# A graph-network layer on one core: moving the on-chip tensors to other start addresses

## The chip, the cores and the metric

The kernel runs on one core of a Trainium2 chip. The metric is the device time of one execution, in microseconds (us). The engines are PE (TensorE; its weight loads are listed as PEld), DVE (VectorE), ACT (ScalarE), POOL (GpSimd) and SP (SyncE, which here only issues DMAs).

## The reference, cut to what matters

```python
h = jnp.maximum(_layernorm(x, axis=-1), 0.0)             # x: [128, 128, 128] f32
# one direction: h1 = h @ W.T ; g = h1 @ Wg.T
#   vals = (h1 + b) * sigmoid(g + bg);  sum over relations of (adj == rel) @ vals
out = fwd(adj, rels 2..40) + bwd(adj.T, rels 2..40) + loop(adj.T, rel 1)
x + relu(out)
```

The adjacency `adj` that is drawn holds only 0 and 1, so that only the loop direction with relation 1 contributes. The kernel computes that direction, sums up on the side how far `adj` is from 0 and 1, and has a general path behind a flag, which is not taken here.

## The kernel before

The 128 graphs (each 128 nodes by 128 features, float32) are worked in 32 groups of 4; two groups are one chunk of 512 KB of x and 512 KB of adj. All of x and all of adj stay on the chip (`x_all`, `adj_all`, 64 KB of each partition each).

The order is written out by hand, one queue for each engine, with semaphores:

- SP issues the loads in order: the first four graphs of x, the two weight matrices, the other four graphs of chunk 0, then x chunks 1 to 3 and adj chunk 0, then x and adj by turns; stores of finished chunks go in between from chunk 8 on. In HBM and in SBUF every run of a transfer is one row of a graph, 512 bytes.
- DVE computes the row statistics (L524), POOL the coefficients (L333, L336, and `rstd` with a power, L339) for batches of one, then two, then four groups. POOL and DVE share the normalisation to `xn` (L352, L541).
- PE transposes `xn` with `ident` (`turn_rows`, L751, 4 steps a group). ACT takes the relu to `hT_hi` (L414), DVE the remainder to `hT_lo` (L567).
- PE multiplies (`products`): for each graph `hT_hi` with `w_hi` (L764) and with `w_lo` (L765), then `hT_lo` with `w_hi` (L769), 12 steps a group, each 256 columns, onto a bias that ACT has put into PSUM (L421).
- ACT takes the sigmoid (L436), DVE multiplies to `vals` (L557), PE sums over the edges (`aggregate`, L786, mask by vals, which show as 8 steps a group), and DVE adds x (L582) in place.
- While it has nothing else to do at the start, PE multiplies `zeros` (`keep_busy`, L716, 256 columns of bf16).

In a PE step the first operand named (`hT`, `xn`, `mask`, `w_raw`) is loaded into the array, and the other (`w_hi`, `w_lo`, `ident`, `vals`, `w_gT`) streams through it. For `zeros` both come from the same tensor.

SBUF tensors are allocated one behind another in the order of the `sb(...)` calls. The program's first one, `x_all`, begins at byte 16,512 of each partition, 128 past a multiple of 4096. As `x_all`, `adj_all`, `xn`, `hT_hi`, `hT_lo`, `gate`, `vals` and `mask` are all multiples of 4096 bytes long, each of them begins 128 past a multiple of 4096. `stats` to `minus_half` take 1600 bytes together, so that `ident`, `ones`, `w_raw`, `w_gT`, `w_hi`, `w_lo`, `bias_all`, `zeros` and `bias_row` begin 192 past a multiple of 512. Every start is a multiple of 64.

Of the kernel before, what the change touches and what calls it, by code (L numbers as in the profile page):

```python
# [6 lines left out]
FP32, FP32R, BF16, INT32 = mybir.dt.float32, mybir.dt.float32r, mybir.dt.bfloat16, mybir.dt.int32  # L7
# [11 lines left out]
def build(nc, x, adj, W_fwd, W_bwd, W_loop, Wg_fwd, Wg_bwd, Wg_loop,  # L19
          b_fwd, b_bwd, b_loop, bg_fwd, bg_bwd, bg_loop, out):  # L20
    B, N, D = x.shape
# [6 lines left out]
    CC = CG * D  # L28
# [16 lines left out]
    with ctx:  # L45
        def sb(name, shape, dt=FP32):
            return ctx.enter_context(nc.sbuf_tensor(name, shape, dt))
# [3 lines left out]

        SIDE = max(B * D, 2 * NREL * D + 36 * D)
        x_all = sb("x_all", [128, SIDE])
        adj_all = sb("adj_all", [128, SIDE], INT32)
        xn = sb("xn", [128, XN, GC])
# [2 lines left out]
        gate = sb("gate", [128, 2, GC])  # L59
        vals = sb("vals", [128, 2, GC])  # L60
        mask = sb("mask", [128, MASKS, GROUP * N])
        stats = sb("stats", [128, BATCH_SLOTS, BATCH // 2, 6])
        var_eps = sb("var_eps", [128, BATCH_SLOTS, BATCH])
        rstd = sb("rstd", [128, BATCH_SLOTS, BATCH])
        mean_neg = sb("mean_neg", [128, BATCH_SLOTS, BATCH])
        minus_half = sb("minus_half", [128, BATCH])
        ident = sb("ident", [128, 128])
        ones = sb("ones", [128, 128])
        w_raw = sb("w_raw", [128, 2, 128])
        w_gT = sb("w_gT", [128, 128])  # L70
        w_hi = sb("w_hi", [128, 2 * D], FP32R)
        w_lo = sb("w_lo", [128, 2 * D], FP32R)
        bias_all = sb("bias_all", [128, 2, D])
        zeros = sb("zeros", [128, 4 * D], BF16)
        bias_row = sb("bias_row", [128, 2, D])
        junk = sb("junk", [128, 4, CC], BF16)
        dist = sb("dist", [128, CHUNKS])
        dist_sum = sb("dist_sum", [1, 1])
        flag = sb("flag", [1, 1], INT32)
# [61 lines left out]
        def view(side, cols):  # L141
            base = x_all[:, :] if side == "x" else adj_f32
            at = room[side]
            room[side] += cols
            assert room[side] <= SIDE
            return base[:, at:at + cols]
# [719 lines left out]
```

How the kernel before makes its waits and increments, by code:

```python
        @block.sync  # L241
# [21 lines left out]
            load_x(1)  # L263
            load_x(2)
            load_x(3)
            load_adj(0)
            for c in range(4, LOAD_AHEAD):
                load_x(c)
                load_adj(c - 3)
            for c in range(LOAD_AHEAD, CHUNKS):
                load_x(c)
                load_adj(c - 3)
                sp.wait_ge(out_ready, (c - LOAD_AHEAD + 1) * CHUNK)
                store_tile((c - LOAD_AHEAD) * CG, (c - LOAD_AHEAD) * CC, CG)
            load_adj(CHUNKS - 3)
            load_adj(CHUNKS - 2)
            load_adj(CHUNKS - 1)
            for c in range(CHUNKS - LOAD_AHEAD, CHUNKS - 2):
                sp.wait_ge(out_ready, (c + 1) * CHUNK)
                store_tile(c * CG, c * CC, CG)
            for g in range(GROUPS - 4, GROUPS - 1):
                sp.wait_ge(out_ready, g + 1)
                store_tile(g * GROUP, g * GC, GROUP)
            sp.wait_ge(out_ready, GROUPS)
            store_tile(B - GROUP // 2, (B - GROUP // 2) * D, GROUP // 2)
            sp.wait_ge(flag_ready, 1)
            with sp.If(sp.value_load(flag[0:1, 0:1], min_val=0, max_val=1) != 0):
                sp.wait_ge(stored, 16 * STORES)
                for d, (b_, bg_) in enumerate(((b_fwd, bg_fwd), (b_bwd, bg_bwd))):
# [10 lines left out]
                with sp.Fori(0, B) as b:  # L302
                    sp.wait_ge(g_stored, b * 16 + 16)
                    sp.dma_start(g_x, x[bass.ds(b, 1), :, :].rearrange("o n d -> n (o d)")
```

## Time and profile before

| | |
|---|---|
| median of 3 runs | 104.76 us (104.61 to 105.29) |
| profiled execution | 104.03 us |
| its span in the profile | 102.2 us, mean granted TensorE clock 0.992 |
| busy | PE 95.4, PEld 91.3, DVE 90.1, ACT 88.6, POOL 85.8 us |
| DMA | 25.45 MB, mean 249 GB/s |

The span goes from the first instruction to the last on the engines; 1.8 us of the execution lie outside it. Busy time is the time in which an engine had at least one instruction under way; steps of PE overlap, so that the distance between two starts is shorter than either step.

### The profile page before, as it was taken

What the parts mean: (1) busy time and instruction counts of PE and PEld (TensorE: products, weight loads), DVE (VectorE), ACT (ScalarE), POOL (GpSimd) and SP (SyncE); (2) the same over time, 40 slices, a digit from 0 to 9 for tenths busy, and PEclk for the clock granted to TensorE, in tenths of its full rate; (3) what the DMA queues carried; (4) which work ended last, traced back from release to release, by engine and by line L of the source; (5) the groups of instructions that cost most, each with busy time, mean ns of one, the idle gap of its engine ahead of it and who ended that gap; (6) DMA issues with size and microseconds to landing.
All of it is one profiled execution on the core that took longest, in us unless ns stands there. A gap on an engine that the chain in (4) does not pass through costs nothing.

```text
span 102.2 us, 2493 instructions
## 1 busy us (share of the span) xinstructions
PE 95.4 (93%) x802; PEld 91.3 (89%) x802; DVE 90.1 (88%) x196; ACT 88.6 (87%) x144; POOL 85.8 (84%) x162
## 2 busy tenths in 40 slices
PE   5986899998999999999999999999999999999960
PEld 2655789797999999999999999999999999999950
DVE  2289989999999999999999999999999788777761
ACT  5075498899799998999899989998999989898990
POOL 2188999999999999999999999999999999991000
PEclk9999999999999999999999999999999999999996
DMA  1899999999999999999999999999945150606345
GB/s 50 242 319 292 290 290 290 291 293 294 293 312 298 328 328 331 311 329 322 333 282 317 271 324 316 327 292 313 345 134 157 58 151 28 184 6 205 103 140 168
DMA packets 50288, 25.45 MB, mean 249 GB/s; under 512 B 866, under 2 KB 50276, under 8 KB 50276
## 3 DMA queue, kind: packets, MB, share of 16 engines
q1 hardware_dynamic: 50000, 25.17, 88.5%
q10 hardware_dynamic: 276, 0.13, 0.4%
q8 instruction: 6, 0.10, 0.4%
q14 instruction: 6, 0.05, 0.1%
HBM read 16.91 MB, written 8.39 MB: 247 GB/s over the span
## 4 chain that ended last, share of the span: by engine, by line
PE 71%; POOL 4%; ACT 3%; issue 1%; DVE 0%; POOLq 0%
PE psum L786 23%; PE psum L764 12%; PE psum L769 12%; PE psum L765 12%; PE psum L751 11%; POOL rstd L339 3%; ACT junk L442 2%; POOL xn L352 1%; ACT gate L436 0%; PE psum L811 0%; DVE dist_sum L628 0%; DVE flag L630 0%; POOLq L362 0%
## 5 line engine op out<-in xcount | busy, mean ns | idle before, releaser
L352 POOL TENSOR_SCALAR xn<-x_all,mean_neg,rstd 128x128 f32<-128x128 f32 x101 | 44.7, 454 | 0.7 <-POOL rstd L339 0.4
L764 PE MATMUL psum<-w_hi,hT_hi 128*128 128x256 f32 x128 | 33.8, 299 | 1.3 <-DVE w_lo L589 0.9
L786 PE MATMUL psum<-vals,mask 128*128 128x128 f32 x256 | 33.6, 275 | 0.1
L421 ACT ACTIVATE psum<-bias_all 128x1024 f32<-128x1024 f32 x32 | 33.1, 1035 | 0.3 <-DVE vals L557 0.3
L786 PEld LDWEIGHTS psum<-vals,mask 128*128 128x128 f32 x256 | 31.0, 191 | 0.2 <-issue 0.2
L765 PE MATMUL psum<-w_lo,hT_hi 128*128 128x256 f32 x128 | 31.0, 277 | 0.0
L524 DVE BATCH_NORM_STATS2 stats<-x_all 128x6 f32<-128x256 f32 x64 | 23.9, 418 | 3.2 <-DMA x_all<-in_x 3.0
L764 PEld LDWEIGHTS psum<-w_hi,hT_hi 128*128 128x128 f32 x128 | 24.1, 188 | 2.0 <-DVE w_lo L589 1.1
L557 DVE TENSOR_TENSOR vals<-psum,gate 128x512 f32<-128x512 f32 (+1 forms) x33 | 21.9, 663 | 3.9 <-ACT gate L436 3.3
L339 POOL TENSOR_TENSOR rstd<-var_eps,minus_half 128x16 f32<-128x16 f32 (+2 forms) x11 | 24.5, 2225 | 0.1
L765 PEld LDWEIGHTS psum<-w_lo,hT_hi 128*128 128x128 f32 x128 | 24.2, 189 | 0.0
L567 DVE SCALAR_TENSOR_TENSOR hT_lo<-psum,hT_hi 128x512 fp32r<-128x512 f32 x32 | 21.8, 682 | 1.2 <-ACT hT_hi L414 1.1
L414 ACT ACTIVATE hT_hi<-psum 128x512 fp32r<-128x512 f32 x32 | 19.2, 600 | 3.5 <-PE psum L751 3.5
L582 DVE SCALAR_TENSOR_TENSOR x_all<-psum,x_all 128x512 f32<-128x512 f32 (+1 forms) x33 | 21.7, 662 | 0.1
L436 ACT ACTIVATE gate<-psum 128x512 f32<-128x512 f32 (+1 forms) x33 | 19.4, 587 | 1.7 <-PE psum L769 1.7
L769 PE MATMUL psum<-w_hi,hT_lo 128*128 128x256 f32 x128 | 20.2, 278 | 0.0
L751 PE MATMUL psum<-ident,xn 128*128 128x128 f32 x128 | 19.5, 275 | 0.7 <-POOL xn L352 0.4
L442 ACT ACTIVATE junk<-adj_all,minus_half 128x1024 bf16<-128x1024 int32 x16 | 18.4, 1153 | 0.0
L769 PEld LDWEIGHTS psum<-w_hi,hT_lo 128*128 128x128 f32 x128 | 17.1, 188 | 0.1
L751 PEld LDWEIGHTS psum<-ident,xn 128*128 128x128 f32 x128 | 14.7, 142 | 1.5 <-POOL xn L352 0.8
L363 POOL CAST mask<-adj_all 128x512 f32<-128x512 int32 x22 | 13.3, 611 | 0.0
L541 DVE TENSOR_SCALAR xn<-x_all,stats,rstd 128x128 f32<-128x128 f32 x27 | 8.7, 340 | 0.0
(36 smaller groups left out, 31.3 us busy)
## 6 DMA issues: line engine op xcount, KB each, us to landing
adj_all<-in_adj SPq DMA_DIRECT2D x16, 512.0 KB, 6.8
x_all<-in_x SPq DMA_DIRECT2D x15, 512.0 KB, 6.8
out<-x_all SPq DMA_DIRECT2D x14, 512.0 KB, 6.2
out<-x_all SPq DMA_DIRECT2D x3, 256.0 KB, 2.3
x_all<-in_x SPq DMA_DIRECT2D x2, 256.0 KB, 3.0
out<-x_all ACTq DMA_DIRECT2D x1, 128.0 KB, 2.5
out<-x_all SPq DMA_DIRECT2D x1, 128.0 KB, 2.6
w_raw<-in_L_gnn_W_loop SPq DMA_DIRECT2D x1, 64.0 KB, 2.5
```

The lines of the kernel that those rows point to most:

```text
L339: pool.tensor_tensor(rstd[:, s, 0:n], var_eps[:, s, 0:n], minus_half[:, 0:n], ALU.pow).then_inc(rstd_ready, 1)
L352: last = pool.tensor_scalar(xn[:, g % XN, j * D:j * D + D], x_all[:, g * GC + j * D:g * GC + j * D + D], mean_neg[:, b % BATCH_SLOTS, k:k ...
L421: nc.scalar.activation(prod_ps[s].rearrange("p g a d -> p g (a d)"), bias_all[:, :, :].rearrange("p a d -> p (a d)").unsqueeze(1) .to_broa ...
L524: last = nc.vector.bn_stats(stats[:, b % BATCH_SLOTS, ((g - first) * GROUP + j) // 2, :], x_all[:, g * GC + j * D:g * GC + (j + 2) * D].re ...
L557: nc.vector.tensor_tensor(per_graph(vals[:, s, :])[:, some, :], prod_ps[s][:, some, 0, :], per_graph(gate[:, s, :])[:, some, :], ALU.mult) ...
L567: nc.vector.scalar_tensor_tensor(out=hT_lo[:, s, :], in0=hT_ps[s], scalar=0.0, in1=hT_hi[:, s, :].bitcast(FP32), op0=ALU.max, op1=ALU.subt ...
L582: nc.vector.scalar_tensor_tensor(out=cols, in0=sums_ps, scalar=0.0, in1=cols, op0=ALU.max, op1=ALU.add).then_inc(half_out if more else out ...
L751: last = nc.tensor.transpose(hT_ps[s][:, j * N:j * N + N], xn[:, g % XN, j * D:j * D + D], ident[:, :])
L764: nc.tensor.matmul(to, hi, w_hi[:, :], start=False, stop=False, skip_group_check=True)
L765: nc.tensor.matmul(to, hi, w_lo[:, :], start=False, stop=False, skip_group_check=True)
L769: last = nc.tensor.matmul(to, lo, w_hi[:, :], start=False, stop=True, skip_group_check=True)
L786: last = nc.tensor.matmul(to[:, j * D:j * D + D], mask[:, g % MASKS, j * N:j * N + N], vals[:, s, j * D:j * D + D], start=True, stop=True)
```

## The change

A tensor of 1920 bytes that nothing reads or writes is put in front, and nine small tensors are allocated right behind `mask` instead of behind the statistics, in another order. No instruction is added, removed or reordered.

```diff
         SIDE = max(B * D, 2 * NREL * D + 36 * D)
+
+        gap = sb("gap", [128, 480])
         x_all = sb("x_all", [128, SIDE])
         adj_all = sb("adj_all", [128, SIDE], INT32)
         xn = sb("xn", [128, XN, GC])
...
         mask = sb("mask", [128, MASKS, GROUP * N])
+        w_hi = sb("w_hi", [128, 2 * D], FP32R)
+        w_lo = sb("w_lo", [128, 2 * D], FP32R)
+        ident = sb("ident", [128, 128])
+        ones = sb("ones", [128, 128])
+        bias_all = sb("bias_all", [128, 2, D])
+        zeros = sb("zeros", [128, 4 * D], BF16)
+        w_raw = sb("w_raw", [128, 2, 128])
+        w_gT = sb("w_gT", [128, 128])
+        bias_row = sb("bias_row", [128, 2, D])
+        junk = sb("junk", [128, 4, CC], BF16)
         stats = sb("stats", [128, BATCH_SLOTS, BATCH // 2, 6])
         var_eps = sb("var_eps", [128, BATCH_SLOTS, BATCH])
         rstd = sb("rstd", [128, BATCH_SLOTS, BATCH])
         mean_neg = sb("mean_neg", [128, BATCH_SLOTS, BATCH])
         minus_half = sb("minus_half", [128, BATCH])
-        ident = sb("ident", [128, 128])
-        ones = sb("ones", [128, 128])
-        w_raw = sb("w_raw", [128, 2, 128])
-        w_gT = sb("w_gT", [128, 128])
-        w_hi = sb("w_hi", [128, 2 * D], FP32R)
-        w_lo = sb("w_lo", [128, 2 * D], FP32R)
-        bias_all = sb("bias_all", [128, 2, D])
-        zeros = sb("zeros", [128, 4 * D], BF16)
-        bias_row = sb("bias_row", [128, 2, D])
-        junk = sb("junk", [128, 4, CC], BF16)
         dist = sb("dist", [128, CHUNKS])
```

By these lengths `x_all` to `mask` and `w_hi` begin 2048 past a multiple of 4096 afterwards, `w_lo` and `w_raw` 3072 past, `ident` and `w_gT` on a multiple of 4096, and `ones`, `bias_all`, `zeros` and `bias_row` on multiples of 512. The statistics and `dist` stay on multiples of 64.

## Rows read from the trace of the kernel before

**Rows 1.** Busy time of each engine by stretch, granted clock, DMA share, GB/s.

```profile
0.00:2.50 2.50, 1.31 (x4) 0.49 (x5) 0.68 (x3) 1.28 (x1) 0.74 (x7) 1.00 0.14 44
2.50:3.70 1.20, 1.20 (x6) 0.71 (x5) 0.07 (x1) 0.00 (x0) 0.00 (x0) 1.00 0.84 244
3.70:5.40 1.70, 1.70 (x10) 1.35 (x8) 0.77 (x3) 0.07 (x1) 0.74 (x2) 1.00 0.87 255
5.40:12.90 7.50, 5.93 (x45) 4.70 (x44) 7.32 (x21) 4.41 (x10) 6.59 (x14) 1.00 1.18 300
12.90:24.60 11.70, 11.16 (x91) 10.32 (x89) 11.29 (x28) 10.98 (x18) 11.02 (x20) 1.00 1.20 292
24.60:45.00 20.40, 20.37 (x181) 20.37 (x182) 20.12 (x43) 19.43 (x33) 20.06 (x36) 1.00 1.12 314
45.00:67.00 22.00, 22.00 (x197) 21.95 (x196) 21.87 (x47) 21.36 (x35) 21.66 (x39) 1.00 1.06 313
67.00:95.00 28.00, 28.00 (x251) 27.99 (x250) 24.16 (x47) 26.84 (x43) 24.99 (x49) 1.00 0.57 165
```

**Rows 2.** Chain that ended last: shares of the span by line.

```profile
by line: PE psum L786 22.7%; PE psum L764 12.2%; PE psum L769 12.1%; PE psum L765 12.1%; PE psum L751 11.4%; POOL rstd L339 2.8%; ACT junk L442 2.1%; POOL xn L352 1.1%; issue 0.7%; ACT gate L436 0.4%; PE psum L811 0.2%; DVE dist_sum L628 0.
```

**Rows 3.** The same chain in time: start, us, what (products L764, L765 left out).

```profile
24.63 0.66 PE psum L751 x4
26.23 0.47 PE psum L769 x4
...
28.97 0.47 PE psum L769 x4
...
58.85 0.45 PE psum L769 x4
59.30 0.89 PE psum L786 x8
60.19 0.44 PE psum L751 x4
61.54 0.45 PE psum L769 x4
...
94.00 0.45 PE psum L769 x4
```

**Rows 4.** Timeline of PE: start, duration of the run of steps.

```profile
6.26 0.60 PE L716 MATMUL psum<-zeros 128*128 128x256 bf16 x4
...
51.90 0.60 PE L751 MATMUL psum<-ident,xn 128*128 128x128 f32 x4
```

**Rows 5.** Who waited for whom: total us, times, longest us.

```profile
POOL var_eps L333 <- DVE stats L524: 3.4, 2, 3.1
...
DVE stats L524 <- DMA x_all<-in_x: 3.0, 2, 2.1
```

**Rows 6.** Timeline of the start: POOL and DVE around the second load.

```profile
4.86 1.03 POOL L339 TENSOR_TENSOR rstd<-var_eps,minus_half 128x4 f32<-128x4 f32 x1
5.33 0.76 DVE L524 BATCH_NORM_STATS2 stats<-x_all 128x6 f32<-128x256 f32 x2 [0.94 <-DMA x_all<-in_x]
6.18 0.21 POOL L333 TENSOR_SCALAR var_eps<-stats 128x4 f32<-128x4 f32 x1 [0.29 <-DVE stats L524]
```

**Rows 7.** The page: GB/s in 40 equal slices, and the queue of all loads and stores (packets, MB, share of 16 DMA engines).

```profile
GB/s 50 242 319 292 290 290 290 291 293 294 293 312 298 328 328 331 311 329 322 333 282 317 271 324 316 327 292 313 345 134 157 58 151 28 184 6 205 103 140 168
...
q1 hardware_dynamic: 50000, 25.17, 88.5%
```

**Rows 8.** DMA issues: KB each, median us from issue to landing.

```profile
out<-x_all SPq DMA_DIRECT2D x1, 128.0 KB, 2.6
```

## Prediction

> **What bounds the kernel now.** I read the busy time by stretch first. In it PE is busy for 20.37 of 20.40 us, then 22.00 of 22.00, then 28.00 of 28.00: from 24.6 us to 95 us PE never runs dry [rows 1]. The chain of work that ended last says the same: 70.5% of the span lies on PE's five lines, 59.1% on those other than the transposes [rows 2]. The chain in time then gives the pitch, the distance from one PE step to the next. A whole group takes 61.54 - 58.85 = 2.69 us, of which 0.44 us are four transposes (0.110 each), 0.45 us the four products of L769 (0.113), 0.89 us the eight steps of L786 (0.111), and the 0.91 us that are left the eight products L764 and L765 (0.114) [rows 3]. There is a second pace: 28.97 - 26.23 = 2.74 us, with 0.47 us for L769, which is 0.1175 a step. Nineteen of the groups in the chain run at the shorter pace; the longer one rules up to 31 us and for two or three groups after a stall of PE. Neither pace follows the address: consecutive groups use the two halves of `hT`, 2048 bytes apart, and hold the same pace.
>
> Before 24.6 us the limit is another one. PE is busy 5.93 of 7.50 and 11.16 of 11.70 us, POOL 6.59 of 7.50 and 11.02 of 11.70 [rows 1]. Nothing but a load holds DVE in front (3.0 us, twice), and through it POOL, which waits 3.4 us for statistics and then has its own queue of powers and normalisations up to the start of the PE-bound stretch [rows 5]. So there are three stretches to price: the start, set by the first loads and then by POOL's queue; the middle, set by PE's pitch; and the end, set by the last store.
>
> **The change part by part.** The instructions, their order and their waits stay. What moves is the start address of every tensor. Each sort of access is one part.
>
> *PE reads.* Before, the streamed `w_hi` and `ident` begin 192 past a multiple of 512 and the loaded `hT`, `xn` and `mask` 128 past one; afterwards all begin on a multiple. If an off-multiple start cost time, steps that have one should be long. The transposes stream `ident` from 192 and load `xn` from 128, and have the shortest pitch of all float32 steps. Four of them take 0.60 us [rows 4]. Four steps that both load and stream `zeros`, from 192, take 0.60 us as well; they stream 256 columns of another type, half as many bytes. With 0.27 us for the last step both come to (0.60 - 0.27) / 3 = 0.11 us. The products are the only ones that stream 1024 bytes in a step, and no row has them at another alignment, so their 0.003 to 0.008 us above that pitch can't be cleared of the address altogether. Bounds: gain of all that lies above the transposes' pitch (rival A), loss of rival B. Between them I take zero, because the rows nearest to it, the transposes and `zeros`, show off-multiple starts at the shortest pitch.
>
> The Trainium skill (SBUF — State Buffer, terms and the note on cachelines) gives 16-byte lines and a penalty for each access that crosses into a new one; every start here is a multiple of 64 before and after. By it PE gains nothing; rival A would go against it. These rows can't separate lines of 16 bytes from longer ones.
>
> *DVE, ACT and POOL accesses.* The starts are multiples of 64 before and after, and in the middle all three are covered by PE. In the start POOL's queue is bare, some 18.4 us from 6.18 to 24.6: one part in a hundred on it would be 0.18 us. No row shows an address at work there; I take zero and keep 0.2 us each way for the range.
>
> *Loads.* `x_all` and `adj_all` move from 128 past a multiple of 256 onto one. In the middle no engine waits for a load, so what is gained there lies under PE. In the start it counts. The load of the other four graphs of chunk 0 ends DVE's wait at 5.33 us; DVE's statistics (0.76 us) end POOL's wait at 6.18 us [rows 6]. POOL had been free since 4.86 + 1.03 = 5.89 us, so 0.29 us can go at once, and more if the first load, which sets that 5.89, comes earlier too. Up to that load 640 KB come in (256, 64, 64, 256). At the 290 GB/s at which the queue runs from 10 to 24 us that is 2.26 us; at 345 GB/s, the best slice of the page, 1.90 us [rows 7]. So the bound of the gain is 0.36 us. The other bound is no gain, as nothing in the trace shows a run of 512 bytes on a multiple. A loss would need a row with loads that suffer from such a start, and there is none; I allow 0.1 us. The queue's average packet took 0.885 x 16 x 102.2 us / 50,000 = 28.9 ns for its 512 bytes. I take 0.25 us, nearer to the gain: in the first 5.4 us the rate is only 244 to 255 GB/s [rows 1], so part of this time is latency that stays. POOL's queue hands such a shift on in full, being filled without a pause up to 24.6 us, and PE hands it on from there.
>
> The rule behind that choice is in the Trainium skill (DMA: Bandwidth & Descriptors, how a descriptor splits into AXI transactions): transactions start on multiples of 256 bytes, and a start between them fetches bytes that go unused. Worked out from it, an estimate: 512 bytes from 128 past a multiple cost 20 beats, from a multiple 16. If the whole packet shrank so, those 2.26 us would become 1.81 us and the gain 0.45 us, before POOL's 0.29 us of slack cuts it. Whether that rule governs writes into SBUF no row shows.
>
> *Stores.* The last one is 128 KB and lands after 2.6 us [rows 8]. At 290 GB/s its bytes are 0.45 us, at 345 GB/s 0.38 us: up to 0.07 us. I take 0.05 us. The earlier stores have landed by then.
>
> *Sum.* On the profiled execution, 104.03 us: 0 - 0.25 - 0.05 gives 103.7 us. The median of the runs is 0.73 us above that execution, so on the median 104.76 - 0.3 = 104.4 us (rounded down).
>
> **The rivals.** *A, PE's pitch falls.* For it: PE is the bound, and the products, whose streamed operand is the longest in bytes, are the slowest steps. Lines L764, L765 and L769 hold 36.4% of the span in the chain, 37.2 us, in 27 groups of 12 = 324 steps, 0.115 us each. At the transposes' 0.110 us they would give back 1.6 us. L786, 22.7% or 23.2 us in 208 steps, 0.1115 each, gives 0.3 us more. With the start's 0.3 us that is 102.5 us; with half of it 103.4 us. Against it: off-multiple starts at the shortest pitch, as shown. From about 0.7 us of it the change is faster by over 1%.
>
> *B, slower: the two operands of a product collide.* Before, `hT` and `w_hi` begin at 128 and 192, so load and stream are 64 bytes apart in phase; afterwards both begin 2048 past a multiple of 4096. If the load and the stream of a step share something by address, steps lose time. The price is bounded by the two paces seen: if the nineteen groups at 2.69 us fall to 2.74 us, that is 0.95 us, and if all 324 products lengthen by the same 0.0045 us, 1.5 us. Less the start's gain it gives 105.4 to 105.9 us. It decides (over 1%) when a product's mean pitch passes 0.119 us. Against it: in L786 `mask` and `vals` already begin at the same phase, 128 past a multiple of 4096, at 0.111 us, and `zeros` loads and streams from one tensor at 0.11.
>
> *C, nothing happens at all:* the loads aren't sped up either, or what they gain is lost to another wait in the start (ACT's for adj, POOL's own queue). Then 104.8 us, give or take the pace of PE: which groups hold 2.74 us changes with each stall, a few groups either way, 0.2 us.
>
> **How the numbers follow.** A run of this kernel can tell about 1% from no change, 1.05 us: said once here. The forecast (start and end gain, PE as it is) has 0.45, C 0.33, A 0.14 (half of it or more 0.12), B 0.08 (past 1% 0.07). The 0.02 of A and the 0.01 of B that are left are within 1%, as are the forecast and C. So faster 0.12, same 0.81, slower 0.07. The likeliest value is 104.4 us. The forecast and C cover 104.4 - 0.45 (all of the load term and POOL's 0.2) to 104.8 + 0.5 (the spread of the runs of before). The range is carried a little into A and B at their half prices: 103.5 to 105.5 us.
>
> **What would show it.** The groups at 2.69 us in the chain of the changed kernel: unchanged against A and B. L769's four steps: 0.44 us would be A, 0.47 us everywhere B. The mean of a queue packet below 28.9 ns and a higher rate between 5 and 24 us confirm the load rule; DVE's wait for x below 3.0 us and the first PE-bound transposes before 24.63 us confirm that it counts. I would be wrong if the products' pitch hangs on where 1024-byte streams begin, or if POOL's queue in the start grows or shrinks with the addresses.

## The result, and the profile after

The changed kernel takes 105.89 us (median of 7 runs, 105.38 to 106.21) against 104.76 us (7 runs); the ratio is 1.0087, 95% interval 1.0064 to 1.011. It is slower by 0.9% (the two medians by themselves lie 1.1% apart), where 0.3% faster had been forecast, and the time lies above the range of 103.5 to 105.5 us. The profiled execution took 106.07 us with a span of 104.3 us, 2.1 us more than the span of before. (Lines of `kernel.py` that stand behind the new allocation are numbered two higher: L764 is L766, L769 is L771.)

Busy time by stretch, columns as in [rows 1]:

```profile
2.50:3.70 1.20, 1.20 (x6) 0.71 (x5) 0.19 (x1) 0.00 (x0) 0.00 (x0) 1.00 0.78 229
3.70:5.40 1.70, 1.70 (x8) 1.27 (x6) 0.57 (x2) 0.00 (x0) 0.86 (x2) 1.00 0.88 256
5.40:12.90 7.50, 6.06 (x45) 4.77 (x44) 7.12 (x21) 5.29 (x11) 6.03 (x13) 1.00 1.14 342
12.90:24.60 11.70, 10.78 (x92) 10.35 (x90) 10.65 (x26) 9.31 (x16) 11.02 (x19) 1.00 1.15 348
24.60:45.00 20.40, 19.84 (x173) 19.65 (x172) 19.94 (x43) 19.14 (x31) 20.06 (x37) 1.00 1.08 317
45.00:67.00 22.00, 22.00 (x194) 22.00 (x192) 21.77 (x47) 21.10 (x35) 21.66 (x40) 1.00 1.07 315
67.00:95.00 28.00, 28.00 (x246) 28.00 (x245) 24.15 (x48) 26.60 (x43) 25.75 (x50) 1.00 0.39 117
```

PE is as full as before from 45 to 95 us, at the same granted clock, and yet gets through fewer steps: 246 instead of 251 from 67 to 95 us. The loads run at 342 and 348 GB/s where they ran at 300 and 292, but not in the first 5.4 us.

The chain that ended last, shares and then pieces in time, to set against [rows 2, 3]:

```profile
by line: PE psum L788 22.3%; PE psum L766 12.5%; PE psum L771 12.4%; PE psum L767 12.3%; PE psum L753 11.1%; POOL rstd L341 2.7%; ACT junk L444 2.1%; POOL xn L354 1.1%; issue 0.7%; ACT gate L438 0.4%; PE psum L813 0.2%; DVE dist_sum L630 0.
...
25.55 0.65 PE psum L753 x4
27.15 0.48 PE psum L771 x4
27.63 0.89 PE psum L788 x8
28.52 0.44 PE psum L753 x4
29.92 0.48 PE psum L771 x4
...
96.32 0.48 PE psum L771 x4
```

Here the 2.1 us can be read off. The first and the last piece with four products of `hT_lo` are 25 groups apart in both kernels: 96.32 - 27.15 = 69.17 us against 94.00 - 26.23 = 67.77 us, **1.40 us** more. That is 2.767 us a group in place of 2.711 on average. There is no short pace any more: four products take 0.48 us in all 26 pieces, while transposes (0.44) and edge sums (0.89) take what they took. The first such piece comes **0.92 us** later, and from the last one to the end it is 104.3 - 96.32 = 7.98 us against 102.2 - 94.00 = 8.2 us, **0.2 us** less. (The 1.40 us are net: the kernel before has 0.12 us of waits at two transposes in this stretch, the changed one none.)

The start, in the timeline (start us, duration us; the last bracket is idle time and what ended it), to set against [rows 6]:

```profile
5.78 0.76 DVE L526 BATCH_NORM_STATS2 stats<-x_all 128x6 f32<-128x256 f32 x2 [1.51 <-DMA x_all<-in_x]
6.63 0.21 POOL L335 TENSOR_SCALAR var_eps<-stats 128x4 f32<-128x4 f32 x1 [0.86 <-DVE stats L526]
12.45 2.06 POOL L354 TENSOR_SCALAR xn<-x_all,mean_neg,rstd 128x128 f32<-128x128 f32 x4 [0.18 <-POOL rstd L341]
13.67 1.16 DVE L543 TENSOR_SCALAR xn<-x_all,stats,rstd 128x128 f32<-128x128 f32 x4
14.60 0.30 POOL L335 TENSOR_SCALAR var_eps<-stats 128x8 f32<-128x8 f32 x1
```

The second load of x ended DVE's wait at 5.78 us, 0.45 us later than before, and POOL's queue (its second run of `var_eps`) began 0.45 us later with it. The other 0.47 us arise inside POOL's queue, mostly between 12.45 and 14.98 us: four pieces of a normalisation take 2.06 us where the kernel before has this:

```profile
11.98 1.74 POOL L352 TENSOR_SCALAR xn<-x_all,mean_neg,rstd 128x128 f32<-128x128 f32 x4 [0.18 <-POOL rstd L339]
13.59 1.10 DVE L541 TENSOR_SCALAR xn<-x_all,stats,rstd 128x128 f32<-128x128 f32 x4
13.80 0.20 POOL L333 TENSOR_SCALAR var_eps<-stats 128x8 f32<-128x8 f32 x1
```

There POOL is done at 13.72 us, 0.13 us after DVE has begun; after the change DVE begins 0.84 us before POOL is done. The queue's share of the page and the time to landing of the last store, to set against [rows 7, 8]:

```profile
q1 hardware_dynamic: 50000, 25.17, 81.1%
...
out<-x_all SPq DMA_DIRECT2D x1, 128.0 KB, 2.3
```

A packet took 0.811 x 16 x 104.3 us / 50,000 = 27.1 ns instead of 28.9.

### The profile page after: what moved, and what is told of

The parts are those of the page before. It is cut to its first block, busy times and chain, and to the rows that moved or that the text cites. A ratio compares the mean times of both kernels' runs of the same rounds, so it can differ in the third digit from the quotient of the medians.

```text
span 104.3 us, 2493 instructions
## 1 busy us (share of the span) xinstructions
PE 97.0 (93%) x802; PEld 93.0 (89%) x802; DVE 90.7 (87%) x196; ACT 88.8 (85%) x144; POOL 86.1 (83%) x162
## 4 chain that ended last, share of the span: by engine, by line
PE 71%; POOL 4%; ACT 2%; issue 1%; DVE 0%; POOLq 0%
PE psum L788 22%; PE psum L766 12%; PE psum L771 12%; PE psum L767 12%; PE psum L753 11%; POOL rstd L341 3%; ACT junk L444 2%; POOL xn L354 1%; ACT gate L438 0%; PE psum L813 0%; DVE dist_sum L630 0%; DVE flag L632 0%; POOLq L364 0%
## 5 line engine op out<-in xcount | busy, mean ns | idle before, releaser
L766 PE MATMUL psum<-w_hi,hT_hi 128*128 128x256 f32 x128 | 34.6, 304 | 0.9 <-DVE w_lo L591 0.6
L788 PE MATMUL psum<-vals,mask 128*128 128x128 f32 x256 | 33.7, 275 | 0.2 <-issue 0.2
L767 PE MATMUL psum<-w_lo,hT_hi 128*128 128x256 f32 x128 | 32.0, 282 | 0.0
L766 PEld LDWEIGHTS psum<-w_hi,hT_hi 128*128 128x128 f32 x128 | 24.2, 189 | 1.5 <-DVE w_lo L591 0.9
L771 PE MATMUL psum<-w_hi,hT_lo 128*128 128x256 f32 x128 | 20.7, 283 | 0.0
L771 PEld LDWEIGHTS psum<-w_hi,hT_lo 128*128 128x128 f32 x128 | 17.7, 192 | 0.0
L543 DVE TENSOR_SCALAR xn<-x_all,stats,rstd 128x128 f32<-128x128 f32 x27 | 9.2, 361 | 0.0
```

The lines of the kernel that those rows point to most:

```text
L766: nc.tensor.matmul(to, hi, w_hi[:, :], start=False, stop=False, skip_group_check=True)
L767: nc.tensor.matmul(to, hi, w_lo[:, :], start=False, stop=False, skip_group_check=True)
L771: last = nc.tensor.matmul(to, lo, w_hi[:, :], start=False, stop=True, skip_group_check=True)
L788: last = nc.tensor.matmul(to[:, j * D:j * D + D], mask[:, g % MASKS, j * N:j * N + N], vals[:, s, j * D:j * D + D], start=True, stop=True)
```

## The experiments

The pace of a group is worked out for each as above, from the first and the last piece of four products in the chain, divided by 25, so that it has in it what PE waits in between; ratios are against runs of the kernel before on the same chip at that time, whose median was 104.31 to 104.76 us.

### Which half of the change, and by what

`again` is the changed kernel once more.

> The changed kernel once more. Known so far: a group of PE steps takes 2.77 us (before: 2.69 or 2.74), four products of hT_lo take 0.48 us (before 0.45 or 0.47), and the stretch that PE bounds begins at 25.5 us (before 24.6). If the pitch belongs to the addresses, the pitch is 0.48 us again in every group. Whether the later start belongs to them too: if it does it begins near 25.5 us again, if it is chance it can be anywhere from 24.5 us on. Time 105.4 to 106.2 us.

Measured: 105.68 us, ratio 1.0131 (1.0083 to 1.0179). The pace is 2.767 us again and 0.48 us in every piece: it belongs to the addresses. POOL's queue began at 6.16 us this time, as before the change, so the 0.45 us of the late load are chance; from there to the first piece of four products (26.59 us) it was 20.43 us, after the change 27.15 - 6.63 = 20.52 us, before 26.23 - 6.18 = 20.05 us. So 0.4 us of the late start are in both traces of this kernel; they come back below, under the start.

That the late load is scatter shows in all the traces: POOL's queue began between 6.16 and 6.75 us in the sixteen with `x_all` moved by the 1920 bytes, and at 6.18 and 6.79 us in the two without.

`gap_only` is the first half of the change alone, `order_only` the second.

```diff
# gap_only, against the kernel before
+        gap = sb("gap", [128, 480])
         x_all = sb("x_all", [128, SIDE])
# order_only, against the changed kernel
-        gap = sb("gap", [128, 480])
         x_all = sb("x_all", [128, SIDE])
```

> Only the 1920 bytes in front, the small tensors in the old order: x_all to mask begin on multiples of 2048, w_hi, w_lo and ident 64 past a multiple of 512. Theory P (the loaded and the streamed operand of a product collide when they begin at the same phase): they are 64 apart, so the short pitch, 0.45 us for four products, about 1.5 us less than the changed kernel, 104.3 us. Theory S (a stream of 1024 bytes that begins on a multiple of 512 is slower by itself): short pitch too, 104.3 us. Theory D (the faster loads, whose targets are now on multiples of 256, disturb PE's reads): the long pitch, 0.48 us, and 105.9 us. All: loads at 340 GB/s or more from 6 to 20 us.

> Only the new order, without the 1920 bytes: everything from x_all to bias_row begins 128 past a multiple of 512, so loaded and streamed operand of a product have the same phase, but none is on a multiple. Theory P: long pitch, 0.48 us for four products, 105.9 us or above. Theory S: short pitch, 0.45 us. Theory D: short pitch, since the loads are as before, near 290 GB/s from 6 to 20 us; for S and D 104.8 us.

`skew64` puts 64 unused bytes ahead of `w_hi` (16 elements; the others called skew likewise).

```diff
+        skew = sb("skew", [128, 16])
         w_hi = sb("w_hi", [128, 2 * D], FP32R)
```

> The changed kernel with 64 more unused bytes ahead of w_hi, so that w_hi to bias_row begin 64 past a multiple of 512 and x_all to mask stay. Theory P and theory S: short pitch, 0.45 us for four products, about 104.3 us. Theory D: long pitch, 0.48 us, 105.9 us.

Measured: `gap_only` 104.35 us (ratio 0.9983, 0.9955 to 1.0011), `skew64` 104.36 us (0.9983, 0.9958 to 1.0008), `order_only` 106.19 us (1.0188, 1.0112 to 1.0264). The chain of `gap_only`:

```profile
90.82 0.44 PE psum L752 x4
92.17 0.45 PE psum L770 x4
...
94.86 0.45 PE psum L770 x4
```

and of `order_only`, with its busy time from 12.9 to 24.6 us:

```profile
92.08 0.44 PE psum L752 x4
93.47 0.48 PE psum L770 x4
...
96.24 0.48 PE psum L770 x4
```

```profile
12.90:24.60 11.70, 11.02 (x93) 10.57 (x92) 10.90 (x26) 10.31 (x17) 11.02 (x20) 1.00 1.20 291
```

94.86 - 92.17 is 2.69 us, 96.24 - 93.47 is 2.77 us. `order_only` has nothing on a multiple of 512 and the old rate of loads, and has the long pace in every group; so neither theory S nor theory D holds. What it shares with the changed kernel is the distance, 0. The whole loss of pace comes from the reordering, none from the 1920 bytes.

### Which tensor

`w64_only` moves `w_hi` and `w_lo` by 64 bytes and puts 448 more behind `w_lo`, so that all that follows moves by 512 and keeps its phase. `rest64` leaves the two where they are and puts the 64 bytes behind them.

```diff
# w64_only, against the changed kernel
+        skew = sb("skew", [128, 16])
         w_hi = sb("w_hi", [128, 2 * D], FP32R)
         w_lo = sb("w_lo", [128, 2 * D], FP32R)
+        back = sb("back", [128, 112])
         ident = sb("ident", [128, 128])
# rest64
         w_lo = sb("w_lo", [128, 2 * D], FP32R)
+        skew = sb("skew", [128, 16])
         ident = sb("ident", [128, 128])
```

> The changed kernel with only w_hi and w_lo moved 64 bytes on; ident, ones, bias_all, zeros and the rest stay on multiples of 512. Theory P (the loaded and the streamed operand of a product collide when they begin at the same phase): short pitch, 0.45 us for four products in most groups, about 104.3 us. Theory R (it is another of the tensors that went along, such as bias_all, which ACT reads, or zeros): long pitch, 0.48 us in every group, about 105.7 us.

> The reverse: w_hi and w_lo stay on multiples of 1024, everything from ident to bias_row moves 64 bytes on. Theory P: long pitch, 0.48 us for four products in every group, about 105.7 us. Theory R: short pitch, about 104.3 us.

Measured: `w64_only` 104.46 us (0.9993, 0.9961 to 1.0026), `rest64` 105.76 us (1.0143, 1.0057 to 1.023). Theory R is out: moving `w_hi` and `w_lo` alone brings the short pace back, moving all that stands behind them doesn't. The chain of `w64_only`, and then of `rest64`:

```profile
92.39 0.45 PE psum L773 x4
95.09 0.45 PE psum L773 x4
```

```profile
93.22 0.48 PE psum L772 x4
...
95.99 0.48 PE psum L772 x4
```

That left one gap: `hT` had not been moved by itself, so the start of `w` alone could have been what counts. `hT64` moves `hT_hi` and `hT_lo` by 64 bytes (4032 bytes ahead of `gate` bring the shift of all that follows to 4096, so that it keeps its phase); `both64` does that and adds the 64 bytes ahead of `w_hi`.

```diff
# hT64, against the changed kernel; both64 has the third line too
+        skew = sb("skew", [128, 16])
         hT_hi = sb("hT_hi", [128, 2, GC], FP32R)
         hT_lo = sb("hT_lo", [128, 2, GC], FP32R)
+        back = sb("back", [128, 1008])
         gate = sb("gate", [128, 2, GC])
...
+        skew2 = sb("skew2", [128, 16])
         w_hi = sb("w_hi", [128, 2 * D], FP32R)
```

> The changed kernel with hT_hi and hT_lo alone 64 bytes on; w_hi and w_lo stay on multiples of 1024. Theory P, distance counts whatever its sign: short pitch, 0.45 us for four products in most groups, 104.4 us. Distance with its sign: w is now 64 behind hT, which with a period of 128 is the same as 64 on, with one of 256 the same as 192 on. Theory W, the start of w by itself counts: long pitch in every group, 0.48 us, 105.7 us.

> The changed kernel with hT_hi and hT_lo 64 bytes on and w_hi to bias_row 64 bytes on: distance zero, and w where it was in the kernels with the short pitch. Theory P: long pitch, 0.48 us in every group, 105.7 us. Theory W: short pitch, 0.45 us, 104.4 us.

Measured: `both64` 105.5 us (1.0084, 1.0043 to 1.0125), `hT64` 104.82 us (1.0011, 0.9968 to 1.0053). The chain of `both64`:

```profile
93.24 0.48 PE psum L774 x4
...
95.99 0.48 PE psum L774 x4
```

and of `hT64`:

```profile
26.93 0.45 PE psum L773 x4
...
95.10 0.47 PE psum L773 x4
```

In `both64` `w` has the phase that it has in `skew64` (it lies 4096 bytes further on), and the pace is 2.754 us instead of 2.717. In `hT64` `w` has the phase that it has in the changed kernel, and the pace is 2.727 instead of 2.767. So the distance of the two counts, and theory W falls. It isn't all that counts: `both64` is at distance 0 and 0.013 us a group short of the other kernels there.

### Which distance

`skew32`, `skew96`, `skew128`, `skew192` and `skew256` have that many bytes ahead of `w_hi` in the place of 64.

> The changed kernel with w_hi to bias_row 256 bytes on, so that loaded and streamed operand are half of 512 bytes apart. Theory P with a period of 512 bytes or more: short pitch, 0.45 us, about 104.3 us. With a period of 256 bytes or less (and over 64): long pitch, 0.48 us, about 105.7 us.

> The changed kernel with w_hi to bias_row 128 bytes on. Known: 64 apart gives the short pitch, 256 apart the long one. Period of 128 bytes: long pitch, 0.48 us for four products in every group, 105.7 us. Period of 256 bytes: short pitch, 0.45 us in most groups, 104.4 us.

> The changed kernel with w_hi to bias_row 32 bytes on. If what counts is that the operands are not in the same 64 bytes of the period, 32 apart still meets for half of the time and gives a pitch between: 0.46 to 0.48 us for four products, 105 us. If any offset that is not a multiple of the period does, short pitch, 0.45 us in most groups, 104.4 us.

> The changed kernel with w_hi to bias_row 96 bytes on. With a period of 128 bytes this is 32 bytes short of a whole one, and as good or bad as 32 bytes on; with a period of 256 bytes it is further apart than 64 and gives the short pitch, 0.45 us in most groups or in all, 104.4 us or a little less.

> The changed kernel with w_hi to bias_row 192 bytes on. Period of 128 bytes: as 64 on, short pitch, 0.45 us, 104.4 us. Period of 256 or more: 192 on is 64 behind, and takes what hT64 takes.

| distance | kernel | pace of a group, us | median us | ratio (95% interval) |
|---|---|---|---|---|
| 0 | after / again | 2.767 / 2.767 | 105.89 / 105.68 | 1.0087 (1.0064 to 1.011) / 1.0131 (1.0083 to 1.0179) |
| 0 | order_only | 2.766 | 106.19 | 1.0188 (1.0112 to 1.0264) |
| 0 | rest64 | 2.767 | 105.76 | 1.0143 (1.0057 to 1.023) |
| 0 | both64 | 2.754 | 105.5 | 1.0084 (1.0043 to 1.0125) |
| 256, so 0 | skew256 | 2.767 | 105.67 | 1.0139 (1.0061 to 1.0217) |
| 32 | skew32 | 2.733 | 104.8 | 1.0006 (0.9974 to 1.0038) |
| 64 | before | 2.711 | 104.76 | 1 |
| 64 | gap_only | 2.703 | 104.35 | 0.9983 (0.9955 to 1.0011) |
| 64 | skew64 | 2.717 | 104.36 | 0.9983 (0.9958 to 1.0008) |
| 64 | w64_only | 2.718 | 104.46 | 0.9993 (0.9961 to 1.0026) |
| 96 | skew96 | 2.767 | 105.76 | 1.0091 (1.0063 to 1.0119) |
| 128 | skew128 | 2.754 | 105.24 | 1.0063 (1.0027 to 1.0099) |
| 192 | skew192 | 2.722 | 104.4 | 0.9995 (0.9966 to 1.0023) |
| -64, so 192 | hT64 | 2.727 | 104.82 | 1.0011 (0.9968 to 1.0053) |

(`gap_wait` below, at distance 64 too, has 2.726.) A distance of 256 gives the pace of 0 to the last digit, so the effect repeats at 256 bytes. That 192 takes nearly what -64 takes, 2.722 and 2.727, would say the same, but only in the mean: in `skew192` 20 of the 25 groups take 2.70 or 2.71 us, every piece of four products 0.45, and waits make up the rest, while in `hT64` every group takes 2.72 or 2.73 without a wait. So where `hT` lies towards the tensors other than `w` matters a little too. It nearly repeats at 128 too: 128 is almost as bad as 0 (2.754 against 2.767), 192 almost as good as 64 (2.722 against 2.717), and between a period of 128 and one of 256 these runs don't decide. What they exclude is that the distance counts without its sign at a period of 128, since 32 and 96 differ (2.733 and 2.767), and that further apart is better: `skew96` was expected at the short pitch or, at the other period, where `skew32` is, and has the long one. `skew32` itself fell between (2.733, and 0.47 us in every piece), as its first expectation said, though its time can't be told from that of before.

### The start

DVE and POOL normalise different groups, each in its own order, without waiting for each other. `skew64_wait` is `skew64` with one wait.

```diff
             row_stats(7)
+            dve.wait_ge(normed_pool, pool_groups(3))
             normalise(3)
```

> The changed kernel with 64 bytes ahead of w_hi and one wait more: DVE begins its normalisation of group 3 only when POOL has done that of group 2. In the kernels with x_all on a multiple of 256, DVE is some 0.4 us earlier there and POOL's last piece takes 0.75 to 0.79 us instead of 0.45. Theory K (the two engines get in each other's way in SBUF, and this eats what the faster loads gain in the start): the piece takes 0.45 us again, PE's bound stretch begins 0.3 to 0.4 us earlier, counted from the landing of the second load of x; 104.0 us. Rival: POOL is slow there for another reason, and the piece stays at 0.75 us or more; then 104.4 us or above, for DVE then starts later.

Measured: 104.01 us, ratio 0.9949 (0.9917 to 0.998). That is 0.3% below the ratio of `skew64`, and the two intervals overlap, so the traces have to show it. POOL's timeline in `skew64`:

```profile
6.36 0.21 POOL L336 TENSOR_SCALAR var_eps<-stats 128x4 f32<-128x4 f32 x1 [0.46 <-DVE stats L527]
12.17 2.07 POOL L355 TENSOR_SCALAR xn<-x_all,mean_neg,rstd 128x128 f32<-128x128 f32 x4 [0.18 <-POOL rstd L342]
```

and in `skew64_wait`, with DVE's next to it:

```profile
6.26 0.21 POOL L336 TENSOR_SCALAR var_eps<-stats 128x4 f32<-128x4 f32 x1 [0.53 <-DVE stats L527]
12.07 1.74 POOL L355 TENSOR_SCALAR xn<-x_all,mean_neg,rstd 128x128 f32<-128x128 f32 x4 [0.18 <-POOL rstd L342]
13.84 1.12 DVE L544 TENSOR_SCALAR xn<-x_all,stats,rstd 128x128 f32<-128x128 f32 x4
```

The four pieces are back at 1.74 us. From the start of POOL's queue to the first piece of four products it is 26.28 - 6.26 = 20.02 us, where `skew64` has 26.80 - 6.36 = 20.44 us and the kernel before 20.05 us. Theory K holds as far as it says that the two engines get in each other's way: 0.33 us is the normalisation, the rest lies in POOL's next instructions. That a DVE instruction which takes the port pair that the two share can shut POOL out of SBUF for its whole length is in the Trainium skill (SBUF — State Buffer, who interferes with whom). The size fits, though no run shows which ports an instruction took: the loss of 0.33 us is about the length of one DVE piece of this kind, 340 ns in the profile of the kernel before:

```profile
L541 DVE TENSOR_SCALAR xn<-x_all,stats,rstd 128x128 f32<-128x128 f32 x27 | 8.7, 340 | 0.0
```

In the kernel after, these DVE pieces are longer too, 361 ns in the mean.

The other half of theory K, that the faster loads bring the two together, isn't shown. `skew256` has the new starts of x and their rate, and no wait added, and yet nothing is lost:

```profile
7.84 1.43 DVE L527 BATCH_NORM_STATS2 stats<-x_all 128x6 f32<-128x256 f32 x4 [0.52 <-DMA x_all<-in_x]
12.00 1.74 POOL L355 TENSOR_SCALAR xn<-x_all,mean_neg,rstd 128x128 f32<-128x128 f32 x4 [0.18 <-POOL rstd L342]
13.85 1.11 DVE L544 TENSOR_SCALAR xn<-x_all,stats,rstd 128x128 f32<-128x128 f32 x4
```

From the start of POOL's queue to the first piece of four products it is 26.15 - 6.20 = 19.95 us, less than before. DVE waited 0.52 us for the third load of x here and came after POOL. So it went in `skew128` and `rest64` too (waits of 0.40 and 0.18 us, four pieces in 1.74 and 1.75 us). In the ten other traces with the new starts and no added wait, DVE didn't wait for that load, and the four pieces took 1.88 us in `skew32` and 2.05 to 2.08 us in the rest. `order_only`, with the old rate, has 1.82 us. So the loss comes only in traces where DVE doesn't wait for the third load; whether the new starts of x make that likelier, these traces can't tell.

`gap_wait` is `gap_only` with the same wait, the old order of the tensors.

> The kernel before with the 1920 bytes in front and the one wait of DVE ahead of its normalisation of group 3, in the old order of the small tensors (w 64 bytes on from hT). Products as before (0.45 us for four in most groups), loads at 340 GB/s, POOL's fourth piece of group 2 back at 0.45 us, last stores 0.3 us sooner: 104.0 us, 0.5 to 0.7 us less than before. If the wait costs as much as it gives, 104.35 us as without it.

Measured: 103.84 us against 104.31 us, ratio 0.9946 (0.992 to 0.9972), in 12 runs. It beats the kernel before by half a per cent, as `skew64_wait` does, and the changed kernel with it; `gap_wait` and `skew64_wait` can't be told apart.

### Edge sums

`mask64_wait` is the changed kernel with the wait and with the 64 bytes ahead of `mask` instead of `w_hi`.

```diff
+        skew = sb("skew", [128, 16])
         mask = sb("mask", [128, MASKS, GROUP * N])
         w_hi = sb("w_hi", [128, 2 * D], FP32R)
```

> The changed kernel with 64 bytes ahead of mask instead of w_hi, and the one wait of DVE: the operands of the products are 64 bytes apart as before, and those of the edge sums (mask loaded, vals streamed), which began at the same phase in every kernel so far, are 64 apart too. Theory P carried over to the edge sums: their pitch goes from 0.1117 to 0.109 us, eight steps from 0.89 to 0.87 us, some 0.5 us in all, 103.5 us. If they don't collide (they stream 512 bytes, read twice, at half the bytes per time of a product): 0.89 us as before, 104.0 us.

Measured: 104.81 us, ratio 1.0018 (0.9995 to 1.0042), 0.8 us above `skew64_wait`. The edge sums take 0.89 us as ever, so their distance doesn't matter to them. But the products lost: 2.742 us a group, 0.47 us in each piece, although their own distance is 64. It is the longer of the two paces of the kernel before, now in every group. So the place of `mask`, which is loaded for other steps of PE's order, has a hand in it too. Why, no run here shows.

## Why the prediction was wrong

- **What bounds the kernel** held: PE for 69 us in the middle (from the first to the last piece of four products), POOL's queue and the first loads in front, the last store behind. All three changed, and all three changes reached the end.
- **PE reads** is the step that failed. I put it at zero because the transposes and `zeros`, which begin off a multiple, have the shortest pitch. That tests the start of a tensor by itself, and indeed it doesn't matter: `order_only`, off every multiple, loses as much pace as the changed kernel. It says nothing of the distance between two operands, and this is what the change altered, from 64 to 0. It cost 1.40 us in the profiled execution, where the sum had 0.
- **Rival B**, the collision, was the right rival, at a chance of 0.08: it hangs on where load and stream lie to each other, though the runs don't show what they share. Its price, bounded by the two paces seen before at 0.95 to 1.5 us, holds the 1.40 us measured. That its time, 105.4 to 105.9 us, holds the 105.89 us too is partly luck: it takes 0.3 us of gain off, and the start gave none. What spoke against it, `mask` and `vals` at one phase with 0.111 us and `zeros` at 0.11, was another sort of step: those stream 512 bytes a step instead of 1024, and `mask64_wait` shows for the edge sums that their distance, 0 or 64, doesn't touch their pitch. I had written myself that no row had the products at another alignment, and still took the value of rows of other kinds.
- **Neither pace follows the address**, read off the halves of `hT`, compared places 2048 bytes apart, a multiple of the 256 bytes after which the effect repeats. It could not have shown anything.
- **Loads**: the rate rose as reckoned, from 292 to 348 GB/s in the full stretch of the start. But the gain of 0.25 us didn't come. Up to 5.4 us the rate is 229 and 256 GB/s, as it was; the second load of x ended DVE's wait at 5.78 us, and POOL's queue began at 6.16 us in the repeat against 6.18 us before: what those bytes wait for isn't the rate of the queue, and no row shows what it is. My allowance for latency should have been all of it.
- **POOL's queue**, which I took as handed on in full, plus or minus 0.2 us for the addresses, grew by 0.47 us in the profiled execution: DVE's normalisation came on top of POOL's. I looked for what an address does to an engine, and what came was one engine beside the other. C spoke of POOL's own queue, but not of DVE beside POOL. It isn't a fixed part of the price: `skew256`, with the same loads, hasn't got it.
- **Stores**: 0.05 us were expected, about 0.2 us came (8.2 to 7.98 us from the last products to the end; 7.94 in `gap_only`, 8.26 in `order_only`, which has no such alignment). Right in sign, too small: the last stores follow one another.
- **Sum**, on the profiled execution: +1.40 pace, +0.45 a late load by scatter, +0.47 within POOL's queue, -0.2 at the end: 2.1 us, the difference of the spans. The medians are 1.1 us apart: the profiled execution of before was 0.73 us under its median, that of the changed kernel 0.18 us over its own.

## What to carry to other kernels

An address of one operand says nothing; set the loaded and the streamed operand of a matmul side by side and ask for their distance, and before a padding "to round numbers" check what distance it undoes. To clear a cause by a row, the row must vary the very quantity that the change varies. And where two engines share a resource without waiting for each other, anything that makes one earlier can make the other late: look at who runs beside whom at the new times.

## What the runs showed of the hardware

- The pitch of matmuls in fp32r, 128 columns loaded and 256 streamed, depends on the distance of the two operands within SBUF modulo 256 bytes: 0.1125 us (0.45 for four, `gap_only` and `skew192`) at best and 0.120 us (0.48) at distance 0 and 96, at a granted clock of 1.00 in these stretches. Float32 transposes don't show it (0.44 us at every distance tried), and edge sums don't at 0 and 64 (0.89 us). The mechanism was not shown: a shared piece of SBUF is an inference. Nor is it the two operands alone: `both64` and `mask64_wait` differ from other kernels at their distance by 0.013 and 0.024 us a group.
- At distance 64 two paces exist side by side, 2.69 and 2.74 us a group, and a stall can switch from one to the other (in the kernel before, four transposes take 0.52 instead of 0.44 us at 46.49 us, and three pieces at 0.47 us follow). With `mask` moved there is only the longer, and at distance 0 there is one pace in each kernel.
- Runs of 512 bytes on a multiple of 256 in SBUF are loaded faster in the stretches where the load queue is full, and not in the first 5.4 us. From 12.9 to 24.6 us a packet took 1.20 x 16 x 512 bytes / 292 GB/s = 33.7 ns before and 1.15 x 16 x 512 / 348 = 27.1 ns after; from 3.7 to 5.4 us it was 27.9 and 28.2 ns. The Trainium skill (DMA: Bandwidth & Descriptors, how a descriptor splits into AXI transactions) has every transaction start on a multiple of 256 bytes; worked out from it, an estimate, such a run costs 20 beats off a multiple and 16 on one, a ratio of 0.80. In this case's traces 27.1 to 33.7 is that ratio in the full stretch, while the light one shows nothing of it, and `order_only` with the old starts keeps 291 GB/s.
- Where DVE's normalisation begins just ahead of POOL's last piece, that piece takes longer: 761 ns instead of 453 in the changed kernel, where DVE begins at 13.67 us and the piece at 13.8. Where DVE begins after POOL's pieces (`skew256`, `skew64_wait`), or within the last one (the kernel before, at 13.59 us, with POOL done at 13.72), POOL loses nothing.
